# TensorE transposes the identity during unit 0's waits in the fill of a four-layer graph kernel

## Chip, core and metric

The kernel runs on one core of a Trainium2 chip. The metric is the device time of one execution in microseconds. Three executions of the kernel before took 1404.98, 1406.11 and 1406.47 us, so its median is 1406.11 us.

## What is computed

The input x holds 128 graphs of 64 nodes with 256 features. One 64x64 adjacency matrix of zeros and ones serves all graphs. Four graph layers follow one another, each added to its input and normalised over the features:

```
x = _layernorm(x + _L0_gnn_ref(x, W, a, beta, adj))      # graph attention, softmax over nodes, elu
x = _layernorm(x + _L1_gnn_ref(x, adj, weight, bias))    # (adj @ x) @ weight + bias
x = _layernorm(x + _L2_gnn_ref(x, w_qkv, ..., adj))      # 8 heads of masked attention
x = _layernorm(x + _L3_gnn_ref(x, adj, adj, ...))        # three steps of a gated recurrent unit
```

## The kernel before

The 128 graphs are cut into 16 units of 512 rows: four tiles of 128 rows, two graphs in each. Each engine has a list of steps written out by hand, and the lists are tied together by semaphores. On every engine the list has three parts: `fill()`, which brings the first units up to the state that the loop expects; `body(i)`, a loop of 11 rounds in which four units are worked on at once, each in another layer; and `drain()`, for the last units. An engine runs its own list strictly in order, so a step that waits holds back all that stands behind it on that engine.

Products in full precision are made of three matrix products of a high and a low part (`matmul3`, L121 to L123). The high part is copied out of PSUM by ScalarE, and the low part is the difference that VectorE takes (L2140).

PSUM's eight banks are two groups of four, `X` (`banks0`) and `Y` (`banks1`). In the fill, unit 0 works in `X` and units 1 and up work in `Y`. The steps of TensorE's fill that matter here are these:

- `l0_turn(u, k)` (L582) turns the input of a unit, four 128x128 transposes into each of banks 0 and 1. `turn_adj` (L565) turns the adjacency matrix.
- `l0_project(u, t)` (L121 to L123, 258 columns) makes layer 0's product for tile t: six matmuls a tile, 24 a unit. It writes columns 0 to 257 of bank t.
- `l0_spread(u)` (L634) hands the attention scores to all nodes. The softmax that follows runs on VectorE and ScalarE (L2172 to L2218).
- `l0_turn_att(u)` (L642) turns the attention matrix, and `l0_attend(u, n)` (L650) multiplies by it, two tiles for each n. It writes banks 2 and 3 in full. VectorE's `l0_add_h(u, n)` (L2227) reads them and increments `s.l0_v`.
- `l1_aggregate(u, k)` (L587) multiplies by the adjacency matrix, and `l1_product(u, t)` (L121 to L123, 256 columns) by layer 1's weights. VectorE's `l1_residual` (L2266) reads the products, two tiles at a time.

`p.ident` is the 128x128 identity. GpSimd makes it at the start (L147 and L153), and TensorE waits for it on the semaphore `made`.

Of the kernel before, what the change touches and what calls it, by code (L numbers as in the profile page):

```python
# [13 lines left out]
P = 128  # L14
PER_TILE = P // NODES
TILES = 4
# [348 lines left out]
def fused(p, block, w, b, s, norms, src, dst, started):  # L365
# [7 lines left out]
    nc = p.nc  # L373
    X, Y = p.ps
# [4 lines left out]
    def is_first(u):  # L379
        return isinstance(u, int) and u == 0  # L380

    def is_second(u):
        return isinstance(u, int) and u == 1
# [4 lines left out]
    def front(u):  # L388
        return X if is_first(u) else Y
# [10 lines left out]
    def x_of(u):  # L400
        return b.own.res if is_second(u) else b.x_tok
# [13 lines left out]
    def columns(t):  # L415
        return slice(t * P, (t + 1) * P)
# [143 lines left out]
    def _(pe):  # L560
        pe.wait_ge(made, 1)

        def turn_adj():
            pe.wait_ge(adj_loaded, 64)
            nc.tensor.transpose(Y[:, TILES - 1, 0:P], adj_blk[:, :], p.ident[:, :]).then_inc(ws["adj_turned"], 1)  # L565
# [14 lines left out]
        def turn(bank, tokens, k):  # L580
            for t in range(TILES):
                ins = nc.tensor.transpose(bank[:, columns(t)], tokens[:, t, k * P:(k + 1) * P], p.ident[:, :])  # L582
            return ins

        def aggregate(bank, tokens, k):
            for t in range(TILES):
                ins = nc.tensor.matmul(bank[:, columns(t)], tokens[:, t, k * P:(k + 1) * P], p.adj_t[:, :],  # L587
                                       start=True, stop=True)
            return ins

        def rows_by_weights(out, of, t, weights, f):
            for k in range(CH):
                ins = matmul3(nc, out, (of[0][:, k, columns(t)], of[1][:, k, columns(t)]),
                              (weights[0][:, k, f], weights[1][:, k, f]), k == 0, k == CH - 1)
            return ins
# [4 lines left out]
        @within  # L600
        def l0_turn(u, k):
            if k == 0:
                if is_first(u):
                    pe.wait_ge(made, 1)
                    pe.wait_ge(s.first_loaded, 16)
                elif is_second(u):
                    pe.wait_ge(s.second_loaded, 16)
                else:
                    pe.wait_ge(*s.loaded.at(u - 2, 16))
                if isinstance(u, int) and u == 2:  # L610
                    pe.wait_ge(*s.l1_lo.at(1, CH))
                    pe.wait_ge(*s.l1_z.at(1, 2))
                elif not isinstance(u, int) or u > 2:
                    pe.wait_ge(*s.f_h.at(u - 2, CH))
                    pe.wait_ge(*s.f_hi.at(u - 2, CH))
                    pe.wait_ge(*s.f_a_lo.at(u - 2, CH))
            turn(front(u)[:, k, :], x_of(u), k).then_inc(s.l0_turned.sem, 1)

        @within
        def l0_project(u, t):  # L620
            if t == 0:
                if is_first(u):
                    pe.wait_ge(ws["l0_ready"], 1)
                if is_second(u):
                    pe.wait_ge(p.const_ready, 1)
                pe.wait_ge(*s.l0_lo.at(u, CH))
            rows_by_weights(front(u)[:, t, 0:WX], b.early, t, w.l0, slice(0, WX)).then_inc(s.l0_h_done.sem, 1)

        @within
        def l0_spread(u):  # L630
            if is_first(u):
                pe.wait_ge(p.const_ready, 1)
            pe.wait_ge(*s.l0_s2_ready.at(u, 1))
            nc.tensor.matmul(front(u)[:, 0, 0:TILES * NODES], p.same_graph[:, :],  # L634
                             b.s2_diag[:, :, :].rearrange("p t j -> p (t j)"),
                             start=True, stop=True).then_inc(s.l0_s2_done.sem, 1)

        @within
        def l0_turn_att(u):
            pe.wait_ge(*s.l0_att_ready.at(u, 1))  # L640
            for t in range(TILES):
                ins = nc.tensor.transpose(front(u)[:, 1, columns(t)], b.att[:, t, :], p.ident[:, :])  # L642
            ins.then_inc(s.l0_att_turned.sem, 1)
# [9 lines left out]
        @within  # L653
        def l1_aggregate(u, k):
            if k == 0:
                pe.wait_ge(*s.y0.at(u, 1))
                if is_second(u):
                    pe.wait_ge(ws["gate_lo"], len(GATES))
                elif not is_first(u):
                    pe.wait_ge(*s.l2_proj.at(u - 1, 2))  # L660
            aggregate(front(u)[:, k, :], b.y0, k).then_inc(s.l1_adj_done.sem, 1)

        @within
        def l1_product(u, t):
            if t == 0:
                if is_first(u):
                    pe.wait_ge(ws["l1_ready"], 1)
                pe.wait_ge(*s.l1_lo.at(u, CH))
            ins = rows_by_weights(half_bank(u, t), l1_parts(u), t, w.l1, slice(0, DIM))
            if t % 2:  # L670
                ins.then_inc(s.l1_out.sem, 1)
# [170 lines left out]
        @within  # L842
        def l3_turn(u, step, n):
            if n == 0:
                pe.wait_ge(*s.h_new.at(u, CH * (step + 1)))
            for t in range(2):
                for k in range(CH):
                    ins = nc.tensor.transpose(rz(u)[:, n, t * DIM + k * P:t * DIM + (k + 1) * P],  # L848
                                              own(u).h[:, k, columns(2 * n + t)], p.ident[:, :])
            ins.then_inc(s.tok_done.of(u), 1)  # L850
# [7 lines left out]
        def body(i):  # L858
# [84 lines left out]
            l3_turn(i, 2, 0)  # L943
            l3_turn(i, 2, 1)

        def fill():
            for n in range(2):
                l0_turn(0, n)
            l0_turn(1, 0)
            turn_adj()  # L950
            l0_turn(1, 1)
            for n in range(4):
                l0_project(0, n)
            l0_spread(0)
            l0_turn_att(0)
            for n in range(2):
                l0_attend(0, n)
            for n in range(4):
                l0_project(1, n)
            l0_spread(1)  # L960
            for n in range(2):
                l1_aggregate(0, n)
            for n in range(4):
                l1_product(0, n)
            l0_turn_att(1)
# [129 lines left out]
        def drain():  # L1095
# [242 lines left out]
            for n in range(2):  # L1338
                l3_turn(15, 2, n)

        run(pe, fill, body, drain)

    @block.scalar
# [1801 lines left out]
```

## Time and profile before

| | |
|---|---|
| median of the three runs | 1406.11 us (1404.98 to 1406.47) |
| time of the profiled execution | 1405.35 us |
| its span, first to last instruction | 1403.2 us |
| mean granted TensorE clock | 0.987 |
| TensorE busy, share of the span | 1337.7 us, 95% |
| VectorE / ScalarE / GpSimd busy | 75% / 56% / 10% |
| chain that ended last | TensorE 68%, VectorE 16%, ScalarE 8%, issue 4%, GpSimd 3% |

2.15 us of the profiled time lie outside the span. In the profile, a row of the timeline gives the start in the span, how long the instructions took together, the engine, the line, what is written and read, and the count; the bracket gives the idle time of that engine just before and what ended it. A matmul's recorded duration is longer than the distance to the next one, because matmuls overlap in the array; the cost of a row of them is therefore read from start to start. The granted clock is 1.00 at 2.4 GHz and 0.50 at 1.2 GHz.

### The profile page before, as it was taken

The numbers are of one execution on the slowest core, as the hardware profiler recorded it, in microseconds if no ns is written. First come the engines' busy times: TensorE is split into PE (matmuls) and PEld (weight loads), VectorE is DVE, ScalarE is ACT, GpSimd is POOL, SyncE is SP. The second block draws the span as 40 slices with busy tenths as digits, with TensorE's granted clock in tenths as the row PEclk, the third lists the DMA queues.
The fourth block names the chain that finished last, engine by engine and source line by source line (L and its number), as shares of the span: only waits on it lengthen the run. The fifth ranks groups of instructions, "written<-read, shape, count | busy, mean of one in ns | idle before, by whom it ended". The sixth has DMA issues, their size and how long they took to land.

```text
span 1403.2 us, 26776 instructions
## 1 busy us (share of the span) xinstructions
PE 1337.7 (95%) x10357; PEld 1134.0 (81%) x10357; DVE 1059.0 (75%) x2367; ACT 791.4 (56%) x1450; POOL 143.4 (10%) x196
## 2 busy tenths in 40 slices
PE   5788999999999999999999999999999999999896
PEld 4677888888888888888888888888888887888784
DVE  5787778787787878778777777878878786868455
ACT  3555565656565565656566655655665555564453
POOL 4200100100010110001011010011001010100000
PEclk9899999999999999999999999999999999999998
DMA  5000010000000001000000001000000100000000
GB/s 174 1 24 24 1 24 31 21 32 15 7 30 22 30 15 37 0 22 30 22 30 15 22 15 22 30 22 30 15 7 30 23 31 9 31 8 31 16 1 30
DMA packets 54653, 34.52 MB, mean 25 GB/s; under 512 B 34896, under 2 KB 51536, under 8 KB 54608
## 3 DMA queue, kind: packets, MB, share of 16 engines
q1 hardware_dynamic: 52800, 29.43, 7.0%
q0 software_dynamic: 1248, 3.94, 0.9%
q8 instruction: 31, 0.51, 0.2%
q10 hardware_dynamic: 560, 0.52, 0.1%
q14 instruction: 14, 0.11, 0.0%
HBM read 12.92 MB, written 8.39 MB: 15 GB/s over the span
## 4 chain that ended last, share of the span: by engine, by line
PE 68%; DVE 16%; ACT 8%; issue 4%; POOL 3%; DMA 0%; ACTq 0%; POOLq 0%; DVEq 0%
PE banks L121 16%; PE banks L123 15%; PE banks L122 15%; PE banks L587 8%; PE banks L582 3%; ACT y L273 2%; PE banks L746 2%; PE banks L650 2%; PE banks L731 2%; PE banks L720 2%; DVE l_stats L245 2%; PE banks L848 1%; DVE l_r L2401 1%; DVE l_r L2394 1%; DVE l_sum L2241 1%
## 5 line engine op out<-in xcount | busy, mean ns | idle before, releaser
L1501 ACT ACTIVATE l_r<-banks,bias_r 128x512 f32<-128x512 f32 x90 | 61.7, 687 | 178.3 <-PE banks L123 178.2
L259 POOL TENSOR_TENSOR l_rstd<-l_mv,eps 128x4 f32<-128x4 f32 x48 | 25.8, 538 | 891.5 <-DVE l_mv L253 891.5
L1518 ACT ACTIVATE banks<-banks,bias_h 128x512 f32<-128x512 f32 x96 | 63.2, 659 | 64.7 <-PE banks L123 64.7
L2140 DVE TENSOR_TENSOR l_rh_lo<-l_r,l_rh_hi 128x512 fp32r<-128x512 f32 x90 | 61.7, 688 | 28.3 <-ACT l_rh_hi L1367 28.1
L2401 DVE SCALAR_TENSOR_TENSOR l_r<-banks,l_r 128x512 f32<-128x512 f32 x90 | 61.7, 687 | 26.4 <-ACT banks L1512 24.6
L1512 ACT ACTIVATE banks<-banks,bias_z 128x512 f32<-128x512 f32 x96 | 63.3, 659 | 26.3 <-PE banks L123 26.2
L273 ACT ACTIVATE y<-l_sum,l_offset,l_rstd 128x256 f32<-128x256 f32 x128 | 70.8, 594 | 12.0 <-DVE l_offset L267 11.1
L587 PE MATMUL banks<-adj_t,y 128*128 128x128 f32 x544 | 72.1, 283 | 4.3 <-ACT y L273 4.3
L587 PEld LDWEIGHTS banks<-adj_t,y 128*128 128x128 f32 x544 | 67.4, 197 | 8.3 <-ACT y L273 5.1
L121 PE MATMUL banks<-l_rh_hi,u_hi 128*128 128x512 f32 x180 | 73.6, 409 | 0.0
L2383 DVE SCALAR_TENSOR_TENSOR l_r<-l_r,l_h 128x512 f32<-128x512 f32 x60 | 40.8, 683 | 41.2 <-ACT l_r L1501 41.2
L122 PE MATMUL banks<-l_rh_hi,u_lo 128*128 128x512 f32 x180 | 71.0, 394 | 0.0
L123 PE MATMUL banks<-l_rh_lo,u_hi 128*128 128x512 f32 x180 | 70.9, 394 | 0.0
L1434 ACT ACTIVATE l_qk<-banks 128x512 f32<-128x512 f32 x64 | 38.2, 599 | 45.0 <-PE banks L123 44.5
L587 PEld LDWEIGHTS banks<-adj_t,l_htok 128*128 128x128 f32 x480 | 56.2, 192 | 6.0 <-ACT l_htok L1367 5.8
L587 PE MATMUL banks<-adj_t,l_htok 128*128 128x128 f32 x480 | 60.1, 278 | 0.8 <-ACT l_htok L1367 0.7
L2140 DVE TENSOR_TENSOR early_lo<-banks,early_hi 128x512 fp32r<-128x512 f32 x62 | 41.0, 684 | 25.9 <-ACT early_hi L1367 25.8
L1367 ACT ACTIVATE l_rh_hi<-l_r 128x512 fp32r<-128x512 f32 x90 | 56.4, 631 | 1.9 <-DVE l_r L2383 1.7
L273 ACT ACTIVATE y<-l_sum,l2o_offset,l2o_rstd 128x256 f32<-128x256 f32 x64 | 33.5, 593 | 41.2 <-DVE l2o_offset L267 41.2
L1367 ACT ACTIVATE early_hi<-banks 128x512 fp32r<-128x512 f32 x62 | 35.3, 598 | 34.9 <-PE banks L582 34.8
L848 PE MATMUL banks<-ident,l_h 128*128 128x128 f32 x360 | 47.9, 276 | 4.5 <-DVE l_h L2407 4.4
L1367 ACT ACTIVATE late_hi<-banks 128x512 fp32r<-128x512 f32 x66 | 37.8, 596 | 24.9 <-PE banks L582 14.2
(294 smaller groups left out, 4354.6 us busy)
## 6 DMA issues: line engine op xcount, KB each, us to landing
x_tok<-in_x_dram SPq DMA_DIRECT2D x15, 512.0 KB, 3.5
l_res<-y SPq DMA_DIRECT2D x15, 512.0 KB, 2.9
out_dram<-l_res SPq DMA_DIRECT2D x15, 512.0 KB, 3.0
l_vpair<-l_vstage SPq DMA_DIRECT2D x32, 128.0 KB, 3.2
w_raw<-in_L_gnn_w_w_dram POOLq DMA_DIRECT2D x3, 512.0 KB, 7.7
qkv_raw<-in_L_gnn_w_qkv_dram POOLq DMA_DIRECT2D x1, 768.0 KB, 4.5
l_res<-in_x_dram SPq DMA_DIRECT2D x1, 512.0 KB, 5.1
u_raw<-in_L_gnn_u_w_dram POOLq DMA_DIRECT2D x2, 256.0 KB, 7.5
```

Of the source, the lines that this page charges most:

```text
L121: nc.tensor.matmul(out, w[0], x[0], start=first, stop=False, skip_group_check=True)
L122: nc.tensor.matmul(out, w[1], x[0], start=False, stop=False, skip_group_check=True)
L123: return nc.tensor.matmul(out, w[0], x[1], start=False, stop=last, skip_group_check=True)
L273: return self.p.nc.scalar.activation(y[:, t, :], z[:, t, :], ACT.Identity, scale=self.rstd[:, t:t + 1], bias=self.offset[:, t:t + 1])
L587: ins = nc.tensor.matmul(bank[:, columns(t)], tokens[:, t, k * P:(k + 1) * P], p.adj_t[:, :], start=True, stop=True)
L848: ins = nc.tensor.transpose(rz(u)[:, n, t * DIM + k * P:t * DIM + (k + 1) * P], own(u).h[:, k, columns(2 * n + t)], p.ident[:, :])
L1367: return nc.scalar.activation(out, source, ACT.Copy)
L1501: nc.scalar.activation(own(u).r[:, m, :], rz(u)[:, m, :], ACT.Tanh, scale=0.5, bias=w.biases["r"][:, m:m + 1]).then_inc(s.r_ready.of(u), 1)
L1512: nc.scalar.activation(rz(u)[:, m, :], rz(u)[:, m, :], ACT.Tanh, scale=0.5, bias=w.biases["z"][:, m:m + 1]).then_inc(s.z_ready.of(u), 1)
L1518: nc.scalar.activation(hv(u)[:, m, :], hv(u)[:, m, :], ACT.Tanh, bias=w.biases["h"][:, m:m + 1]).then_inc(s.hv_ready.of(u), 1)
L2140: return nc.vector.tensor_tensor(parts[1][:, k, :], bank, parts[0][:, k, :].bitcast(F32), ALU.subtract)
L2401: nc.vector.scalar_tensor_tensor(own(u).r[:, m, :], rz(u)[:, m, :], 1.0, own(u).r[:, m, :], ALU.add, ALU.mult).then_inc(s.step.of(u), 1)
```

## The change

Only TensorE's fill is touched. A new helper issues n 128x128 transposes of the identity. They all write to the same place, which nothing reads: columns 384 to 511 of bank 3 of `X`. The result is never used. With `behind_layer_0` TensorE first waits until VectorE has read unit 0's attention output (both halves of `l0_add_h(0, n)`), since `l0_attend` fills that bank completely. The helper is called seven times, with 12, 5, 3, 18, 6, 14 and 8 transposes, 66 in all. No other engine, queue or buffer is touched.

```diff
+        def keep_busy(n, behind_layer_0=False):
+
+            if behind_layer_0:
+                pe.wait_ge(*s.l0_v.at(0, 2))
+            for _ in range(n):
+                nc.tensor.transpose(X[:, TILES - 1, 3 * P:4 * P], p.ident[:, :], p.ident[:, :])
+
         def fill():
+            keep_busy(12)
             for n in range(2):
                 l0_turn(0, n)
+            keep_busy(5)
             l0_turn(1, 0)
             turn_adj()
             l0_turn(1, 1)
+            keep_busy(3)
             for n in range(4):
                 l0_project(0, n)
             l0_spread(0)
+            keep_busy(18)
             l0_turn_att(0)
             for n in range(2):
                 l0_attend(0, n)
             for n in range(4):
                 l0_project(1, n)
+            keep_busy(6, behind_layer_0=True)
             l0_spread(1)
+            keep_busy(14, behind_layer_0=True)
             for n in range(2):
                 l1_aggregate(0, n)
+            keep_busy(8, behind_layer_0=True)
             for n in range(4):
                 l1_product(0, n)
```

## Rows read from the trace of the kernel before

**Rows 1.** Busy time by stretch, the loop: us, each engine's busy us (instructions), PEclk, DMA.

```profile
117.00:1298.00 1181.00, 1166.61 (x9140) 989.74 (x9135) 914.93 (x2053) 687.53 (x1262) 107.80 (x140) 1.00 0.07 21
```

**Rows 2.** Busy time by stretch, the fill; columns PE, PEld, DVE, ACT, POOL, PEclk, DMA share, GB/s.

```profile
5.30:15.60 10.30, 7.68 (x33) 6.92 (x34) 6.88 (x21) 2.60 (x5) 6.58 (x11) 1.00 0.78 215
15.70:22.50 6.80, 1.77 (x11) 1.19 (x10) 3.61 (x10) 3.20 (x7) 3.84 (x6) 1.00 0.91 332
22.52:29.30 6.78, 5.69 (x17) 4.55 (x18) 4.43 (x8) 1.23 (x2) 0.00 (x0) 0.50 0.03 8
29.40:36.10 6.70, 3.12 (x22) 2.51 (x21) 5.24 (x15) 3.25 (x6) 2.79 (x4) 1.00 0.26 79
36.20:49.80 13.60, 9.54 (x43) 9.27 (x44) 11.67 (x18) 3.61 (x7) 5.71 (x6) 0.50 0.01 1
```

**Rows 3.** Timeline of TensorE's matmuls in the fill, unit 0's part.

```profile
5.37 1.94 PE L582 MATMUL banks<-ident,x_tok 128*128 128x128 f32 x8 [5.37 <-DMA x_tok<-in_x_dram]
9.04 1.12 PE L582 MATMUL banks<-ident,l_res 128*128 128x128 f32 x4 [1.74 <-DMA l_res<-in_x_dram]
...
12.04 0.58 PE L121 MATMUL banks<-l_w_hi,early_hi 128*128 128x258 f32 x1 [0.81 <-DVE l_w_lo L2080]
...
16.53 0.28 PE L123 MATMUL banks<-l_w_lo,early_hi 128*128 128x258 f32 x1
17.90 0.67 PE L634 MATMUL banks<-l_s,same_graph 128*128 128x256 f32 x2 [1.10 <-DVE l_s L2166]
22.92 1.11 PE L642 MATMUL banks<-ident,l_att 128*128 128x128 f32 x4 [4.35 <-DVE l_att L2218]
24.72 3.78 PE L650 MATMUL banks<-l_h,l_att_t 128*128 128x256 f32 x8 [0.69 <-ACT l_att_t L1367]
...
29.50 0.28 PE L121 MATMUL banks<-l_w_hi,early_hi 128*128 128x258 f32 x1
...
31.54 0.28 PE L123 MATMUL banks<-l_w_lo,early_hi 128*128 128x258 f32 x1
33.69 0.70 PE L634 MATMUL banks<-l_s,same_graph 128*128 128x256 f32 x2 [1.86 <-DVE l_s L2166]
38.24 3.78 PE L587 MATMUL banks<-adj_t,y 128*128 128x128 f32 x16 [3.86 <-ACT y L273]
44.05 0.55 PE L121 MATMUL banks<-l_w_hi,late_hi 128*128 128x256 f32 x1 [2.02 <-DVE late_lo L2140]
...
49.09 0.41 PE L123 MATMUL banks<-l_w_lo,late_hi 128*128 128x256 f32 x1
```

**Rows 4.** The same timeline later, the same kinds of matmul at the full clock.

```profile
50.85 1.99 PE L650 MATMUL banks<-l_h,l_att_t 128*128 128x256 f32 x8 [0.69 <-ACT l_att_t L1367]
...
73.42 1.07 PE L582 MATMUL banks<-ident,x_tok 128*128 128x128 f32 x8 [0.41 <-DVE l_sum L2266]
...
86.27 0.66 PE L642 MATMUL banks<-ident,l_att 128*128 128x128 f32 x4
```

**Rows 5.** Timeline of the other engines where they set a bound, 1 to 50 us.

```profile
1.57 0.29 POOL L153 TENSOR_SCALAR_AFFINE_SELECT ident<-ident 128x128 f32<-128x128 f32 x1 [0.26 <-POOL minus_half L151]
...
18.45 0.63 ACT L1359 ACTIVATE proj_hi<-proj_raw 128x512 fp32r<-128x512 f32 x1 [1.15 <-DMA ln_beta<-in_L_gnn_ln_beta_dram]
...
18.98 0.58 ACT L1367 ACTIVATE early_hi<-banks 128x512 fp32r<-128x512 f32 x1
...
20.90 0.42 ACT L1386 ACTIVATE l_e<-l_e 128x256 f32<-128x256 f32 x1 [1.33 <-DVE l_e L2196]
...
28.54 0.75 DVE L2227 SCALAR_TENSOR_TENSOR l_v<-l_h,l_beta,banks 128x512 f32<-128x512 f32 x1 [0.23 <-PE banks L650]
...
49.62 0.69 DVE L2266 TENSOR_TENSOR l_sum<-banks,l_sum 128x512 f32<-128x512 f32 x1 [1.67 <-PE banks L123]
```

**Rows 6.** Busy time by stretch where TensorE ran transposes and little else; columns as in Rows 2.

```profile
54.50:58.20 3.70, 3.35 (x28) 3.02 (x28) 3.38 (x6) 3.44 (x8) 0.00 (x0) 1.00 0.00 0
1302.30:1306.00 3.70, 3.66 (x18) 3.66 (x19) 0.69 (x1) 2.51 (x5) 0.00 (x0) 0.54 0.35 142
```

## The prediction, made before the change was run

> **What bounds the kernel now.** I read the table of busy time by stretch first. In the loop TensorE is busy 1166.6 of 1181 us at the full clock [rows 1], so time saved in the loop has to come from TensorE, and every microsecond by which the fill ends earlier moves the whole loop forward. The fill is different. TensorE waits there for VectorE, ScalarE and two loads, and the same table shows its clock [rows 2]: 1.00 recorded up to 22.5 us, 0.50 from 22.5 to 29.3, 1.00 to 36.1, 0.50 from 36.2 to 49.8. Third comes TensorE's timeline [rows 3], for the waits and for the distance from matmul to matmul. It shows that the first record of the clock can't be trusted: 24 projection matmuls of 258 columns go from 12.04 to 16.53 us, 23 steps in 4.49 us, while 17 steps of the same shape take 2.04 us (0.12 each) between 29.50 and 31.54 at the recorded 1.00. At 1.2 GHz a step of nearly that shape costs (49.09 - 44.05) / 23 = 0.219 us. So the first projection ran at the low level for about 16 of its 24 matmuls, whatever the record says. Both recorded falls follow a time in which TensorE did little: 3.9 us without work in the stretch before 22.5, and only two matmuls (0.70 us) between 31.8 and 36.2. The two rises come at the end of long work.
>
> **What the change adds.** 66 transposes. At the low clock eight took 1.94 us and four 1.12, so one more costs (1.94 - 1.12) / 4 = 0.21 us; at the full clock (1.07 - 0.66) / 4 = 0.10 us [rows 3, 4]. Each group stands ahead of a wait that is there anyway. The count by the wait that covers it:
> - 12 ahead of the first input: the identity is ready at 1.86 us [rows 5] and the input ends the wait at 5.37. 12 x 0.21 = 2.5 us, with a tail of some 0.3 they end by 4.7. Covered.
> - 5 ahead of unit 1's input: 1.1 us at the low clock against 1.74. Covered.
> - 3 ahead of the projection: 0.63 against 0.81. Covered by only 0.18 us.
> - 18 ahead of the turned attention: 3.8 us low, 1.8 us full, against 4.35. Covered.
> - 6 ahead of the second spread: 1.3 or 0.6 against 1.86. Covered.
> - 14 ahead of the aggregation: 2.9 or 1.4 against 3.86. Covered.
> - 8 ahead of layer 1's product: 1.7 or 0.8 against 2.02. Covered.
>
> The three new waits are for VectorE's second `l0_add_h`, which ends at 29.3 us [rows 5]. The first of them stands behind a projection that ends after 31.5, so it is over before it is reached; the other two ask for the same value. What is queued behind it is the second spread and everything of TensorE after it. I cost all of this at nothing. If a cover went, the excess would fall on the chain one for one.
>
> **What the change takes away.** The low clock, where TensorE's work is on the chain. Step by step, if the clock rises before 12 us and holds:
> - Projection of unit 0: 16 matmuls become shorter by 0.219 - 0.12 = 0.1 us, 1.6 us. Not all of it arrives. ScalarE's exponential at 20.90 stands behind the weight split at 18.45, which waits for a load, and behind the copy at 18.98, which ends at 19.56 [rows 5]. The exponential can come forward by 1.3 us only. Gain 1.3.
> - Turned attention: 4 transposes, 1.11 us against 0.66 [rows 3, 4]. Gain 0.45.
> - Attention product: 3.78 us against 1.99 [rows 3, 4]. VectorE takes the two halves in turn. The first half would be there about 1.0 us after the start, and VectorE needs 0.75 us for it and 0.7 for the step behind it before it can take the second: 2.5 us after the start instead of 28.54 - 24.72 = 3.8. Gain 1.3.
> - Projection of unit 1 and aggregation: 0 here. After the aggregation VectorE, not TensorE, ends the wait at 44.05. The 1.8 us by which the aggregation gets shorter become wait.
> - Layer 1's product: 24 matmuls, 5.0 us, would be 2.8 us. VectorE idled 1.67 us for its end, at 49.62 [rows 5], and is then bound by its own list. Gain 1.65.
>
> Sum: 1.3 + 0.45 + 1.3 + 1.65 = 4.7 us. After 50 us the clock is full in both kernels and the rest of the fill moves rigidly.
>
> **What speaks against the full sum.** The filler is sized for the low clock. Once the clock is up, 18 transposes fill 1.8 us of a wait of 4.35, and TensorE idles 2.5 us, turns the attention in 0.66 and waits 0.69 again. After the shorter aggregation the last wait grows to 2.0 + 1.8 = 3.8 us, and 8 transposes fill 0.8: 3.0 us idle. The trace has falls after 3.9 us of nothing and after 0.70 us of work in 4.4 us, and no fall after 1.7 us of nothing ahead of 54.5. My two gaps lie between these. A fall at the first puts the gains of the turn and the product of attention at risk, 1.75 us; a fall at the second, the 1.65 of layer 1's product. In each case I expect the clock back part-way through, so I take one fall at half its price, 0.85 us. That gives 4.7 - 0.85 = 3.85 us.
>
> **A rule that speaks against the change.** From 54.5 to 58.2 us TensorE ran 28 transposes and nothing else, after 1.6 us idle, and the clock stayed at 1.00. From 1302.3 to 1306.0 it ran 18 instructions, two thirds of them transposes, at 0.54 on average, and was at 1.00 again right after [rows 6]. The Trainium skill, page "TensorE: Matmul & The Clock Gate", section "Part 4: PE-mode transpose", says that the full clock doesn't engage for transposes, because they don't count as busy in the same way. By that rule the 66 transposes would leave the clock as it is and the sum would be 0; these rows speak for transposes that do count, at least to hold the clock. The rise in the second row had matmuls mixed in, so the rule isn't excluded for a rise from nothing, which is what the first group of 12 asks for.
>
> **The rivals, with their times** (profiled execution 1405.35 us, 0.76 us under the median of 1406.11, so I subtract from the median):
> - Forecast: the clock rises early and is lost at most once and briefly. Gain 3.1 to 4.7, at 3.85: 1402.3. Chance 0.55.
> - The start stays at the low clock or both gaps lose it: some 1.0 to 3.0 us of the 4.7 arrive, at 2.0: 1404.1. For it: when TensorE's clock changes can't be read off beforehand, and the record starts only at 15 us. Chance 0.23.
> - Transposes don't raise or hold the clock: the covers hide all, 1406.1. Against it, rows 6. Chance 0.12. This is also the case in which the change doesn't do what it says.
> - Slower: transposes into one and the same place run one after the other instead of overlapping. No row shows transposes with one target. Each would then cost what the first of a row costs, 1.12 - 3 x 0.21 = 0.5 us at the low and 0.66 - 3 x 0.10 = 0.36 at the full clock. It decides from 4.35 / 18 = 0.24 us each, where the wait ahead of the turned attention is full. The first, third and fourth group at 0.5: 12 x 0.5 end at 7.9 instead of 5.37, +2.5; 3 x 0.5 - 0.81, +0.7; 18 x 0.5 - 4.35, +4.65. The last three at 0.36: +0.3, +1.2, +0.9. Sum 10.2 us, less at most 4.7 gained: 1411.6. Against it: the three matmuls of a product accumulate into the same columns and follow each other at 0.12 us all the same. Chance 0.06. Some 0.04 is left for what I don't see.
>
> **How the numbers follow.** Predicted 1402.3. The lower end takes the full sum and 1.2 us more, because the runs of before differ by 1.5 us among themselves and the time before the first projection could shrink a little too: 1400.2. The upper end goes to the middle of what lies between the second case and no change, 1405.4, and leaves out the cases of no change and slower, and what of the second lies beside them. For this kernel 0.2% is 2.8 us, about what a measurement can tell from no change. In the forecast nearly all is above that (0.51 of 0.55), in the second case little (0.06 of 0.23). Faster 0.57, same 0.35, slower 0.08.
>
> **What the profile of the changed kernel would show.** The first projection's 23 steps at 0.12 us, 2.9 us in all; the spread at 16.4 instead of 17.9 us, the turned attention near 21.6, the aggregation near 35, layer 1's product near 41, VectorE's second residual near 45 instead of 49.6. TensorE's waits ahead of these steps end by the same releasers as before; where one ends by nothing but TensorE itself, a group was too long. A clock at 0.50 anywhere between 9 and 50 us shows a gap that the filler didn't cover. The prediction is wrong if the clock pattern is that of before, if the transposes stand more than 0.24 us apart, or if the time won by 50 us is no longer there at 117 us.

## The result, and the profile after

Twenty-one executions of each kernel gave a median of 1404.07 us for the change (1401.16 to 1406.20) and 1405.97 us for the kernel before (1403.64 to 1407.19). The ratio is 0.9987, with a 95% interval of 0.9981 to 0.9993. That is 1.9 us less by the medians and 1.8 by the ratio, half of the 3.85 us that were forecast. It is clear of no change, but less than the 0.2% (2.8 us) from which the prediction called it faster. The profiled execution took 1404.12 us, with a span of 1402.0 us against 1403.2.

The busy time by stretch, cut where the clock of the kernel after changes, answers to [rows 2] (us, busy us of PE, PEld, DVE, ACT, POOL, then PEclk, DMA share, GB/s):

```profile
12.00:15.20 3.20, 3.15 (x24) 2.94 (x24) 2.25 (x14) 1.50 (x4) 3.20 (x5) 1.00 1.12 288
15.60:21.20 5.60, 2.64 (x20) 2.33 (x20) 3.16 (x9) 1.97 (x5) 4.02 (x6) 1.00 0.92 335
21.30:28.40 7.10, 5.63 (x18) 4.51 (x19) 4.73 (x9) 1.23 (x2) 0.00 (x0) 0.52 0.16 57
28.50:38.20 9.70, 6.13 (x50) 5.55 (x49) 8.30 (x18) 5.38 (x10) 5.64 (x6) 1.00 0.17 55
38.40:41.70 3.30, 3.30 (x16) 3.00 (x15) 3.23 (x5) 1.20 (x2) 2.59 (x4) 0.50 0.00 0
41.90:51.90 10.00, 5.82 (x37) 4.88 (x38) 8.94 (x24) 2.36 (x5) 1.23 (x2) 1.00 0.00 0
52.00:55.40 3.40, 3.40 (x18) 3.40 (x17) 2.42 (x5) 2.22 (x6) 0.00 (x0) 0.50 0.02 5
```

There are three falls of the clock instead of two, and the third, at 52 us, is new. The recorded time at the low level is shorter all the same: 7.1 + 3.3 + 3.4 = 13.8 us against 6.8 + 13.6 = 20.4 us. The record has its first entry at 15.7 us in the kernel before and at 7.6 us here. The time ahead of it, which the view prints as 1.00, isn't in these sums. TensorE's timeline says which work was caught. It answers to [rows 3], and L951 is the new helper:

```profile
1.91 2.82 PE L951 MATMUL banks<-ident 128*128 128x128 f32 x12 [1.91 <-POOL ident L153]
5.35 1.94 PE L582 MATMUL banks<-ident,x_tok 128*128 128x128 f32 x8 [0.61 <-DMA x_tok<-in_x_dram]
7.08 0.96 PE L951 MATMUL banks<-ident 128*128 128x128 f32 x5
9.12 0.66 PE L582 MATMUL banks<-ident,l_res 128*128 128x128 f32 x4 [1.08 <-DMA l_res<-in_x_dram]
...
12.01 0.39 PE L121 MATMUL banks<-l_w_hi,early_hi 128*128 128x258 f32 x1 [1.36 <-DVE l_w_lo L2094]
...
14.88 0.28 PE L123 MATMUL banks<-l_w_lo,early_hi 128*128 128x258 f32 x1
16.26 0.67 PE L634 MATMUL banks<-l_s,same_graph 128*128 128x256 f32 x2 [1.10 <-DVE l_s L2180]
16.77 2.13 PE L951 MATMUL banks<-ident 128*128 128x128 f32 x18
22.09 1.12 PE L642 MATMUL banks<-ident,l_att 128*128 128x128 f32 x4 [3.19 <-DVE l_att L2232]
23.89 3.78 PE L650 MATMUL banks<-l_h,l_att_t 128*128 128x256 f32 x8 [0.69 <-ACT l_att_t L1381]
...
37.24 2.85 PE L587 MATMUL banks<-adj_t,y 128*128 128x128 f32 x16 [2.33 <-ACT y L273]
39.88 1.91 PE L951 MATMUL banks<-ident 128*128 128x128 f32 x8
43.04 0.36 PE L121 MATMUL banks<-l_w_hi,late_hi 128*128 128x256 f32 x1 [1.24 <-DVE late_lo L2154]
...
46.27 0.66 PE L642 MATMUL banks<-ident,l_att 128*128 128x128 f32 x4 [0.17 <-DVE l_att L2232]
...
51.80 0.95 PE L576 MATMUL banks<-ident,u_raw 128*128 128x128 f32 x4 [2.18 <-DVE l_v L2241]
...
56.82 0.47 PE L121 MATMUL banks<-late_hi,qkv_hi 128*128 128x512 f32 x1
```

The projection ran at the full clock, 23 steps in 2.87 us. The 18 transposes were over at 18.9 us, TensorE then idled 3.19 us, the clock fell, and the turned attention and its product took 1.12 and 3.78 us, as before. Layer 1's product ran at the full clock. The lines from 46.27 us on are unit 1's turned attention, the first transpose of the gate weights and the first matmul of layer 2's projection. In the kernel before, the same three were:

```profile
49.31 0.86 PE L642 MATMUL banks<-ident,l_att 128*128 128x128 f32 x4
...
54.56 0.63 PE L576 MATMUL banks<-ident,u_raw 128*128 128x128 f32 x4 [1.72 <-DVE l_v L2227]
...
58.67 0.48 PE L121 MATMUL banks<-late_hi,qkv_hi 128*128 128x512 f32 x1 [0.36 <-DVE late_lo L2140]
```

So the fill had won 3.04 us at the first of them, 2.76 at the second and 1.85 at the third. The span had won only 1.2 at its end. To see where the rest went I compared the start of the mask matmuls (L709, once for each unit) in the two traces: the kernel after is ahead by 1.83 us at the first, by 2.07 at the fourteenth, and by 1.29 at the fifteenth. Below, this difference is called the lead. Between the last two TensorE's timeline has a wait that the kernel before doesn't have:

```profile
1109.31 0.50 PE L121 MATMUL banks<-f_h_hi,u_hi 128*128 128x512 f32 x1
1110.31 0.50 PE L122 MATMUL banks<-f_h_hi,u_lo 128*128 128x512 f32 x1 [0.50 <-issue]
```

The second matmul comes 1.00 us behind the first, instead of 0.33, with the clock at 1.00 and nothing that the profile shows as awaited.

### The profile page after: what moved, and what is told of

It reads as the page before. It is cut to its first block, busy times and chain, and to the rows that moved or that the text cites. A ratio compares the mean times of both kernels' runs of the same rounds, so it can differ in the third digit from the quotient of the medians.

```text
span 1402.0 us, 26908 instructions
## 1 busy us (share of the span) xinstructions
PE 1343.0 (96%) x10423; PEld 1139.1 (81%) x10423; DVE 1059.1 (76%) x2367; ACT 790.7 (56%) x1450; POOL 143.3 (10%) x196
## 4 chain that ended last, share of the span: by engine, by line
PE 68%; DVE 16%; ACT 7%; issue 4%; POOL 3%; DMA 1%; SPq 0%; ACTq 0%; POOLq 0%; DVEq 0%
PE banks L121 16%; PE banks L123 15%; PE banks L122 15%; PE banks L587 8%; PE banks L582 3%; PE banks L746 2%; ACT y L273 2%; PE banks L650 2%; PE banks L731 2%; PE banks L720 2%; DVE l_stats L245 2%; PE banks L848 1%; DVE l_r L2415 1%; DVE l_r L2408 1%; DVE l_sum L2255 1%
```

## The experiments

All times are medians, set against the kernel before on the same chip in the same rounds; "by the ratio" is the ratio's distance from 1, in us of the kernel before. The two differ by up to 0.7 us; the executions of one kernel often lie in two groups. The lead is that of one profiled execution. It is not exact late in the loop: in the profiles of two kernels that come out of the fill with no lead (the short control and the 36 transposes alone, below) it drifts to 0.4 and 0.5 us by 1109 us. The kernels that bear the change's groups differ from the kernel after only as their diff says.

**Front and back alone.** Which groups bring the gain?

```diff
             for n in range(4):
                 l0_project(0, n)
             l0_spread(0)
-            keep_busy(18)
             l0_turn_att(0)
...
-            keep_busy(6, behind_layer_0=True)
...
-            keep_busy(14, behind_layer_0=True)
...
-            keep_busy(8, behind_layer_0=True)
```

> Only the first three groups (12, 5, 3 transposes), all ahead of unit 0's first projection. Theory (the gain comes from a higher clock for the work that is on the chain, each stretch for itself): the projection's 24 matmuls stand 0.12 us apart, the first spread comes at about 16.3 us instead of 17.9, and the time falls by 0.8 to 1.5 us, since a weight load still bounds ScalarE; the clock then falls as before ahead of the turned attention. Rival (the groups only work together, because the clock is lost again in the first uncovered wait and everything behind comes out as before): within 0.3 us of the kernel before.

Measured: 1404.93 against 1406.23 us, ratio 0.9987 (0.9978 to 0.9996), 1.3 us by the medians and 1.8 by the ratio. Five executions took 1403.0 to 1403.7 us and six 1404.9 to 1405.6. The theory's size fits the medians; its mechanism, each stretch for itself, doesn't fit the profile, which is one of the faster five. There the lead is 1.01 us at the spread and 1.32 ahead of layer 1's product, and 2.44 behind it: the clock came back at 40.7 us, so a part of that product ran at the full clock with no filler ahead of it. In this execution the clock had risen during the first projection (steps of 0.21 us up to 13.3 us, of 0.12 from 13.5), and the spread came at 16.89 us. The same twelve, five and three transposes gave a rise before 9.1 us in the profile of the change and after 13 here, so the start is not the same in every execution.

The other half leaves out the groups of 12, 5 and 3:

```diff
         def fill():
-            keep_busy(12)
...
-            keep_busy(5)
...
-            keep_busy(3)
```

> Only the last four groups (18, 6, 14, 8). Theory: the projection is as before (23 steps in about 4.5 us, 17.9 us for the spread); what is gained is in the attention product and layer 1's product, 0.5 to 2.5 us depending on whether the clock is lost in the half-filled waits. With the first three groups' gain it adds up to that of the whole change, 1.9 us. Rival (the whole gain is in the first projection): within 0.3 us of the kernel before.

Measured: 1406.14 against 1406.23 us, ratio 0.9994 (0.9986 to 1.0003). Between 0.1 us by the medians and 0.8 by the ratio; I can't tell it from no gain, so the last four groups, 46 of the 66 transposes, bring little as they are, though three of the eleven executions took 1403.7 to 1403.8 us. The trace shows why it is less than nothing in the profiled one. The lead of 0.98 us at the first transpose of the gate weights fell to 0.17 with a fall of the clock at 54.4 us, and then the clock fell at 82 us, where it hadn't fallen in the profile of the kernel before. TensorE's timeline there, and behind it the twelve transposes in the kernel before:

```profile
80.09 0.70 PE L634 MATMUL banks<-l_s,same_graph 128*128 128x256 f32 x2 [1.05 <-DVE l_s L2177]
...
81.96 2.82 PE L731 MATMUL banks<-ident,l_prob 128*128 128x128 f32 x12 [1.16 <-ACT l_prob L1465]
```

```profile
82.12 1.70 PE L731 MATMUL banks<-ident,l_prob 128*128 128x128 f32 x12 [1.16 <-ACT l_prob L1454]
```

The twelve transposes took 2.82 us instead of 1.70, and by the mask matmuls this execution lost 0.95 us between 72 and 105 us. The same loss of about 1 us, at the same step, is in three more profiles below (the first covered fill, the overlong control, the moved split).

**Groups sized for the full clock.** Does the missing half lie in the half-filled waits?

```diff
-            keep_busy(3)
+            keep_busy(10)
-            keep_busy(18)
+            keep_busy(40)
-            keep_busy(6, behind_layer_0=True)
+            keep_busy(14, behind_layer_0=True)
-            keep_busy(14, behind_layer_0=True)
+            keep_busy(32, behind_layer_0=True)
-            keep_busy(8, behind_layer_0=True)
+            keep_busy(32, behind_layer_0=True)
...
+            pe.wait_ge(*s.l1_z.at(0, 2))
+            keep_busy(18)
             for n in range(2):
                 turn_gate(n)
```

> The groups sized for the full clock: 12, 5, 10, 40, 14, 32, 32, and an eighth of 18 ahead of the first turned gate weight. Theory (the change loses more than half of the 4.7 us that a steady clock is worth, because its groups end early at the full clock): granted clock without a fall from 9 to 60 us, second residual of layer 1 near 45 us, time 3.5 to 5 us under the kernel before and the runs closer together than the change's 5 us. Rival (the sum was too large, since VectorE and the weight loads bound the fill anyway): no fall of the clock but a gain under 2.5 us. Second rival (the longer groups end behind the wait they cover and hold the chain up): TensorE's waits at 22, 33, 37 and 43 us end by TensorE itself, gain under 1 us.

Measured: 1402.43 against 1406.23 us, ratio 0.9971 (0.9960 to 0.9983), 3.8 us. After the projection there is no clock below 1.00 up to 60 us; it fell at 79.5 us, and the lead went from 3.34 to 2.28 us. The second rival was right for one group: those ten transposes ahead of the projection met the low clock, took 2.34 us from 11.35 on, and the spread came at 18.15 us, later than before. So I put the third group back to 3 and filled the first two waits better:

```diff
-            keep_busy(12)
+            keep_busy(15)
-            keep_busy(5)
+            keep_busy(8)
-            keep_busy(10)
+            keep_busy(3)
```

> The groups sized for the full clock again (now 15, 8, 3, 40, 14, 32, 32 and the eighth of 18); the third stays at 3. In the run with 12, 5 and 10 the clock came up only after 12 us, the third group ended behind its wait at the low clock, and the first spread came at 18.15 us. Theory (the clock's rise comes too late when the first two waits are filled only in part): the transposes at 9 us stand 0.1 us apart, the first spread comes at 16.3 us, the second residual near 44.7, and the time is 4 to 5.5 us under the kernel before, 0.5 to 1.5 under that run. Rival (when the clock rises is not in the filler's hands): the spread stays at 17.9 in the profile and the time is within 0.5 us of that run.

Measured: 1400.55 against 1405.19 us, ratio 0.9971 (0.9962 to 0.9980), 4.6 us by the medians and 4.1 by the ratio. By the ratio that is no more than the run before it, and the two ran on different chips, so the times don't decide between theory and rival; the profile has what the theory named, the spread at 16.26 us. This is the fill with a steady clock. One stretch says it, and in the timeline every long group ends just ahead of the end of the wait that it covers:

```profile
9.00:60.00 51.00, 43.74 (x325) 39.58 (x326) 42.08 (x100) 22.55 (x45) 21.12 (x28) 1.00 0.27 85
```

```profile
16.77 4.53 PE L951 MATMUL banks<-ident 128*128 128x128 f32 x40
21.84 0.65 PE L642 MATMUL banks<-ident,l_att 128*128 128x128 f32 x4 [0.54 <-DVE l_att L2234]
23.18 1.99 PE L650 MATMUL banks<-l_h,l_att_t 128*128 128x256 f32 x8 [0.69 <-ACT l_att_t L1383]
...
41.08 0.36 PE L121 MATMUL banks<-l_w_hi,late_hi 128*128 128x256 f32 x1 [0.27 <-DVE late_lo L2156]
...
49.84 0.63 PE L576 MATMUL banks<-ident,u_raw 128*128 128x128 f32 x4 [0.22 <-DVE l_v L2243]
...
53.94 0.47 PE L121 MATMUL banks<-late_hi,qkv_hi 128*128 128x512 f32 x1 [0.35 <-DVE late_lo L2156]
```

Layer 2's projection starts at 53.94 instead of 58.67 us: 4.73 us, where the prediction's full sum was 4.7. The span is 1398.4 us, 4.8 less.

**Activity, or only instructions?** The first control keeps the 66 instructions and the three waits and takes the work away:

```diff
-                nc.tensor.transpose(X[:, TILES - 1, 3 * P:4 * P], p.ident[:, :], p.ident[:, :])
+                nc.tensor.matmul(X[:, TILES - 1, 3 * P:3 * P + 8], p.ident[:, :], p.ident[:, 0:8], start=True, stop=True)
```

> The same 66 instructions in the same places and the same three waits, each a matmul of 8 columns instead of a transpose of 128. Theory (it is TensorE's activity that raises the clock, not the instructions or the waits): the clock's pattern and the time are those of the kernel before, within 0.5 us. Rival (something in the order or in the waits brings the gain): 1.5 to 2.5 us under the kernel before, as the change.

Measured: 1409.50 against 1406.23 us, ratio 1.0024 (1.0015 to 1.0033), 3.3 us slower. Neither expectation. Each of these matmuls is two in the trace and costs about 0.44 us at the low clock, so several groups ran over their waits, the first among them:

```profile
1.91 5.29 PE L951 MATMUL banks<-ident 128*128 128x8 f32 x24 [1.91 <-POOL ident L153]
```

The first group ended at 7.2 us, where the input had landed at 5.3. That makes it a measurement of the slower rival instead: what a filler costs when it is longer than its wait. The input's transposes came 1.7 us late and the spread 1.8. The profiled execution was 3.6 us behind at 72 us; it lost 1.1 more in a fall at 86 us and 0.3 in a standstill (see the end). With half as many (6, 3, 1, 9, 3, 7, 4), added to the kernel before, the control is a control:

> Matmuls of 8 columns again, half as many (6, 3, 1, 9, 3, 7, 4), since each took two instructions of 0.22 us and the groups ran over their waits. TensorE is then recorded as busy in the same waits for about as long as with the transposes at the low clock, but moves few columns. Theory (what counts for the clock is work such as a full transpose does, not that TensorE has instructions): first spread at 17.9 us as before, clock at 0.50 for as long as before, time within 0.5 us of the kernel before. Rival (any instructions in the waits do it): 1.5 to 2.5 us under the kernel before, like the change.

Measured: 1406.29 against 1405.58 us, ratio 1.0005 (0.9996 to 1.0014): no gain. TensorE's rows look filled, and the work behind them ran at the old level:

```profile
1.90 2.73 PE L951 MATMUL banks<-ident 128*128 128x8 f32 x12 [1.90 <-POOL ident L153]
...
18.07 0.67 PE L634 MATMUL banks<-l_s,same_graph 128*128 128x256 f32 x2 [1.10 <-DVE l_s L2180]
18.58 3.00 PE L951 MATMUL banks<-ident 128*128 128x8 f32 x18
23.09 1.12 PE L642 MATMUL banks<-ident,l_att 128*128 128x128 f32 x4 [1.51 <-DVE l_att L2232]
24.89 3.78 PE L650 MATMUL banks<-l_h,l_att_t 128*128 128x256 f32 x8 [0.69 <-ACT l_att_t L1381]
```

The clock was at 0.50 from 19.5 to 29.7 and from 36.6 to 50.2 us. So it is the transposes' work that raises the clock, not instructions in TensorE's rows.

**The load that caps the first gain.** The weight split moves behind the turned attention on ScalarE:

```diff
-            high_proj()
             l0_high(1, 0)
             l0_exp(0)
             l0_high(1, 1)
             l0_take_att(0)
+            high_proj()
```

> The change as it is, and on ScalarE the split of the projection weights of layer 2, which waits for a load until 18.5 to 19.1 us, stands behind the copy of the turned attention instead of ahead of unit 0's exponential. Theory (that wait caps what the first three groups bring at 0.8 to 1.3 us): where the first projection runs at the full clock the exponential comes at 19.3 us instead of 20.1, and the time falls 0.5 to 0.8 us below that of the change. Rival (the cap costs nothing, because the clock lost in the wait behind decides): no difference from the change within 0.3 us.

Measured: 1403.20 against 1405.19 us, ratio 0.9982 (0.9973 to 0.9991), 2.0 us, against the change's 1.9. The mechanism is in the trace. The exponential, at 20.90 us before [rows 5], came behind the load at 20.08 us in the change and at 19.21 us here:

```profile
19.06 0.63 ACT L1373 ACTIVATE proj_hi<-proj_raw 128x512 fp32r<-128x512 f32 x1 [3.40 <-DMA ln_beta<-in_L_gnn_ln_beta_dram]
...
20.08 0.41 ACT L1400 ACTIVATE l_e<-l_e 128x256 f32<-128x256 f32 x1
```

```profile
19.21 0.42 ACT L1400 ACTIVATE l_e<-l_e 128x256 f32<-128x256 f32 x1 [3.11 <-DVE l_e L2210]
```

In time, though, it can't be told from the change (2.5 us by the ratio, against 1.8, with intervals that overlap). In its profile the wait behind the 18 transposes was shorter, 2.39 us instead of 3.19, and the clock held through it; it fell at 30.5, 40.7 and 51.0 us instead:

```profile
22.57 2.00 PE L650 MATMUL banks<-l_h,l_att_t 128*128 128x256 f32 x8 [0.69 <-ACT l_att_t L1381]
```

By the mask matmuls this execution was ahead by 3.63 us at 72 us, by 2.68 at 105 (the clock had fallen at 78.3 us) and, after an unexplained wait of 0.84 us at 1109, by 1.64 at 1260.

**One wait, or the later waits.** Starting from the change, once only the fourth group is lengthened:

```diff
-            keep_busy(18)
+            keep_busy(40)
             l0_turn_att(0)
```

> The change with the fourth group, ahead of the turned attention, at 40 instead of 18. Theory (each half-filled wait puts its own stretch at risk, and the half price taken in the prediction was too low for this one): no fall of the clock at 19 to 24 us where the start ran at the full clock, the attention product in 2.0 us instead of 3.8 in most executions, 0.5 to 1.5 us under the change. Rival (the clock only moves its fall to the next half-filled wait and the sum stays): no gain on the change.

Measured: 1404.54 against 1405.58 us, ratio 0.9993 (0.9984 to 1.0002), 1.0 us, which can't be told from no gain over the kernel before: the rival's time. The group did its work, the attention product took 2.00 us, and the clock then fell three times behind it, at 31.4, 41.7 and 51.9 us, in the waits still half filled. The lead was 2.60 us at 72 us. Then TensorE stood still three times without a reason in the profile (1.02, 0.71 and 0.47 us of idle), and 0.36 us were left:

```profile
74.40 0.33 PE L720 MATMUL banks<-l_qk 32*64 32x64 f32 x3 [1.02 <-issue]
```

Once only the later groups are lengthened (14, 32, 32, and the eighth of 18):

> The change with the first four groups as they are and the later ones at 14, 32, 32 and an eighth of 18. Theory: aggregation, layer 1's product and the transposes at 51 us at the full clock whatever came before, 0.8 to 2 us under the change; together with the run with the long fourth group about what the fully covered fill gained on it (2.2 to 2.7 us). Rival (nothing behind 30 us is on TensorE's account, VectorE bounds it): within 0.3 us of the change.

Measured: 1403.87 against 1405.58 us, ratio 0.9986 (0.9977 to 0.9995), 1.7 us, the change's gain. Here the clock fell at 22.2 us and never again in the fill, the lead at 72 us was 3.37 us, 1.5 more than the change's, and 0.7 of it went in one such standstill (1.07 us at 104 us). So both halves raise the lead at the end of the fill in their profiles, by 0.8 and 1.5 us over the change's, and neither shows in the median. I expected the two to add up to the covered fill's 2.2 to 2.7 us over the change; in the medians they don't, and the one that covers everything does.

**The end of the kernel.** The wait of 3.96 us at 1298 us, filled in the kernel before and alone:

```diff
+            for _ in range(36):
+                nc.tensor.transpose(Y[:, TILES - 1, 3 * P:4 * P], p.ident[:, :], p.ident[:, :])
             for n in range(2):
                 l3_turn(14, 0, n)
```

> The kernel before with only the 36 transposes near the end. Theory: the eight transposes behind the wait take 1.07 us instead of 1.83, no clock of 0.50 between 1298 and 1306 us, gain 0.8 to 1.8 us. Rival (bounded by VectorE and ScalarE): no gain, within 0.3 us.

Measured: 1403.60 against 1405.19 us, ratio 0.9990 (0.9981 to 0.9999), 1.6 us by the medians. By the profile it is 0.9: the span is 1.46 us shorter, but 0.56 of it was there at 1260 us, ahead of the transposes. The first row is the busy time of the last stretch, with no fall of the clock (0.91 in the change's profile). The second is the eight transposes behind the wait, and in the fence behind it stand the same eight in the kernel before:

```profile
1290.00:1310.00 20.00, 19.98 (x130) 17.56 (x129) 15.55 (x41) 10.93 (x21) 2.47 (x4) 1.00 0.21 80
```

```profile
1301.74 1.09 PE L848 MATMUL banks<-ident,l_h 128*128 128x128 f32 x8
```

```profile
1302.34 1.83 PE L848 MATMUL banks<-ident,l_h 128*128 128x128 f32 x8 [3.96 <-DVE l_h L2407]
```

**All of it together:** the covered fill, the moved split, the 36 transposes.

> The groups of the run before this one, the moved weight split, and 36 transposes ahead of the one long wait of TensorE near the end (3.96 us at 1298 us in the kernel before, behind which 18 instructions ran at the low clock). Theory (each part gives back what the low clock took on the chain, and the parts add up): 5.5 to 7.5 us under the kernel before, the fastest of all. Rival (the last wait lies beside VectorE's and ScalarE's work, which bounds the end anyway): within 0.5 us of the run with the long groups and the moved split alone, so 4.5 to 5.5 us under the kernel before.

Measured: 1399.59 against 1405.19 us (1398.98 to 1399.83 in 5 executions), ratio 0.9960 (0.9946 to 0.9974), 5.6 us. It is the fastest kernel here: 1.0 us under the covered fill, at the foot of what the theory said. The rival, nothing from the last wait, doesn't fit its trace, where the span is 1396.8 us and the lead of 5.54 us at 1260 us grows to 6.4.

**Why one kernel's executions differ by 3 us.** The covered fill's eleven executions fell into six at 1399.7 to 1400.6 us with a mean clock of 0.994 or 0.995, and five at 1401.7 to 1403.1 with 0.992. One more group covers one of the two waits at 80 us. (A group ahead of the spread as well would write a bank that ScalarE still reads, so no kernel with both was timed.)

```diff
             l0_spread(2)
+            for _ in range(10):
+                nc.tensor.transpose(Y[:, TILES - 1, 3 * P:4 * P], p.ident[:, :], p.ident[:, :])
```

> The kernel of the covered fill (15, 8, 3, 40, 14, 32, 32, 18) and one more group of 10 transposes behind unit 2's spread, where TensorE waits 1.16 us at 80 us (the wait of 1.05 us ahead of the spread stays open). In three of the profiles the clock fell there and the same steps took 1.0 us longer, in the others not. Theory (the second, slower half of that kernel's executions, 1401.7 to 1403.1 against 1399.7 to 1400.6, are those that lose the clock there): the slower half is gone, all executions within 1 us at about 1400.2, 4.7 to 5.2 us under the kernel before. Rival (the slower half comes from the start, where the transposes may or may not raise the clock in time, or from the supply of instructions): both halves are still there, time within 0.5 us of that kernel.

Measured: 1400.70 against 1405.34 us, ratio 0.9963 (0.9949 to 0.9977), all five executions between 1400.3 and 1400.9 at 0.994 or 0.995. That is 4.6 us under the kernel before and what the theory says. If nothing had changed, all five would fall into the lower group with a chance of about (6/11)^5, 5%. It isn't shown all the same: this ran on another chip, and the full version above, which has no such group, has five executions within 0.9 us and a clock of 0.994 or 0.995 as well. None of the slower executions of the covered fill has a profile.

## Why the prediction was right, and where it was too large

**Right: the covers.** All seven groups ended ahead of what they cover; each wait behind them still ends by the releaser of before. Twelve transposes with one target took 2.82 us at the low clock and eighteen 2.13 at the full one, (2.82 - 0.4) / 11 = 0.22 and (2.13 - 0.3) / 17 = 0.11 us apart. So they overlap like any others, and the rival that they don't is out. Its price was real, though: the overlong control cost 3.3 us.

**Right: the sum with a steady clock.** 4.7 us were worked out, and 4.73 measured at the start of layer 2's projection in the covered fill, with a median 4.6 us lower. The terms hold there one by one. The lead is 1.08 us at the turned attention, 1.54 at its product and 2.97 ahead of the aggregation and of layer 1's product, and 4.72 at the first transpose of the gate weights. That is 1.08, 0.46, 1.43 and 1.75 us for terms of 1.3, 0.45, 1.3 and 1.65. In the change the first came to 0.8: the weight split behind the load started at 19.06 us instead of 18.45. The steps that the prediction put at 16.4, 21.6, 35 and 41 us came at 16.26, 21.84, 35.27 and 41.08 us in the covered fill.

**Right in direction, too small in size: the risk of losing the clock again.** This is the term that was mis-sized. I saw that the groups were sized for the low clock and that idle stretches of 2.5 and 3.0 us would be left, and took one fall at half its price, 0.85 us. In the profiled execution the clock fell in the first, at 21 us, and at the full price: the turn and the product of attention gave nothing of their 1.75 us, and the lead ahead of layer 1's product was 1.01 us against 2.97 in the covered fill. The second gap didn't open. The clock fell at 38 us already, in the aggregation, behind a wait of 2.33 us that I had only counted as covered. That cost nothing on the chain, as TensorE still waited 1.24 us for VectorE behind it, and layer 1's product then ran at the full clock. In three other profiles (the back groups, the moved split, the long fourth group) the second gap did open, 2.9 us of idle, and the clock fell in each behind it. There half the price was right: 0.85 us of the 1.75 arrived. All half-filled waits together cost 4.6 - 1.9 = 2.7 us by the medians, instead of 0.85.

**Missed: falls behind waits that the prediction didn't price.** The wait of 2.2 us at 49.6 us was 1.7 before the change; a wait of 2.4 us had passed without a fall in the moved split. In the change the clock fell behind it, and 18 transposes ran at half speed. This took the lead from 2.76 to 1.85 us, 0.9 us that the prediction had at nothing: "After 50 us the clock is full in both kernels". The three profiles just named lost 0.8 us at the same place. In the profiled execution this and the first fall are the whole miss at the end of the fill: 2.0 us less than the covered fill up to 51.8 us (0.25 of it the later load), and 0.9 behind. The same kind of loss is in the stretch at 78 to 86 us, in four of the experiments' profiles. Moving the fill by a microsecond or two changes which gap is hit.

**A sign of being wrong that came.** The prediction named itself wrong "if the time won by 50 us is no longer there at 117 us". 3.0 us were won at 46 us and 2.8 at 52, and 1.9 were left at 105. So the measured time lies inside the stated range because the range was wide, not because the path was the one described.

**Missed: not every microsecond of the fill arrives.** I let the lead pass through the loop unchanged. In the covered fill it did (4.71 us at the second unit's mask matmuls, 4.95 at the last). In the change 0.8 us went at 1109 us, without a clock change, and in five more profiles 0.3 to 2.5 us went the same way.

**The rule on transposes.** The profiles speak against it for a rise from nothing as well: up to 9.1 us TensorE had done only transposes, and the next four took 0.66 us, the time at the full clock. In the profile with the later groups lengthened it had done only the first twelve, and the eight behind them took 1.07 us, the full clock's time again:

```profile
5.50 1.07 PE L582 MATMUL banks<-ident,x_tok 128*128 128x128 f32 x8 [0.77 <-DMA x_tok<-in_x_dram]
```

In the covered fill 40 transposes held 1.00 for 4.5 us. What the Trainium skill's page says of transposes ("TensorE: Matmul & The Clock Gate", "Part 4: PE-mode transpose") isn't what this chip did with fp32 ones.

**The chances.** The time is that of the second case, "some 1.0 to 3.0 us of the 4.7 arrive", at 1404.1, and I gave it 0.23 because the gaps looked like a detail of the first. That it fits to 0.03 us is luck: in the profiled execution neither of its conditions held, since the start ran at the full clock and one of the two gaps lost it, not both. The upper end of the range, 1405.4, doesn't follow either; the middle between 1404.1 and no change is 1405.1. The result lies inside both.

## What to carry to other kernels

A filler must be sized for the clock that it brings about: transposes that fill a wait at 1.2 GHz fill half of it at 2.4, and the half left open can undo the gain, so the first groups want to be short (an overlong one of 5.3 us at the low clock delayed the input's transposes by 1.7) and the later ones long. Price a gap by the work behind it on the chain, fill all gaps of the stretch or expect the fall in the next one, and judge by many executions, since single executions of one kernel differ by more than the change brings (1401.2 to 1406.2 us here).

## What was not expected of the hardware

The time of an execution follows the mean granted clock closely. Of the change's 21 executions, the six at 0.992 took 1401.16 to 1402.67 us and the three at 0.988 took 1405.56 to 1406.20. The kernel before isn't one number either. In 93 executions it has a mean of 1406.4 us at 0.985 (31 of them) and 1405.0 at 0.987 (21).

TensorE's standstills without a releaser (0.5 to 1.3 us of idle, in the change, the moved split, the two partly lengthened kernels and both controls, at 74, 104, 113, 198, 1110 and 1192 us among other places) are in no profile of the kernel before, of the front or back groups alone, of the covered fills, of the 36 transposes alone or of the full version. The clock was 1.00 at 1110 us. All eight have one thing in common: a load of instructions (queue q8, 16 KB) had started 1.6 to 2.2 us before TensorE stopped, and TensorE went on 2.3 to 3.1 us after that start. In six of the eight the load fell among some 2000 small packets of another transfer, in the change that of `l_vpair`. The queues from 1107.5 to 1109.8 us in the change's profile:

```profile
q1 hardware_dynamic: 2011, 0.25, 73.0%
q8 instruction: 1, 0.02, 3.0%
```

Most such loads pass without a standstill (31 in the kernel before, none of them with one), some of those among as many packets too. So a TensorE that waits for its instructions fits all eight, but no run tested it. Whether the longer instruction list brings it about, and why the covered fills are free of standstills, stays open.

A matmul of 8 columns in fp32 is two instructions of 0.22 us each in the trace at the low clock and of about 0.11 at the full one ((1.62 - 0.73) / 8 between groups of 14 and 6), each as long as a whole 128-column transpose at the same clock, and leaves TensorE recorded as busy while the clock stays low.
